# Transposes of W_down dealt out over the first two pairs of rows, with ScalarE's copies and two of GpSimd's steps at other places

## The reference

```
xn = layernorm(x)
s  = attention(xn, Wq, bq, Wk, bk, Wv, bv, gamma)
q4(t): per block of 16: scale = max|t| / 6; nearest of 0, .5, 1, 1.5, 2, 3, 4, 6 (with sign) * scale
h  = silu(q4(xn) @ q4(w_gate).T) * (q4(xn) @ q4(w_up).T)      # 704 wide
g  = silu(q4(h) @ q4(w_down).T)
out = x + s * g
```

## Time and profile before

| | before |
|---|---|
| median of 3 runs | 601.14 us (600.61 to 601.36) |
| the profiled execution | 601.82 us, of which its span is 599.7 us |
| TensorE (PE) busy | 549.6 us, 92% of the span |
| VectorE (DVE) busy | 557.2 us, 93% |
| ScalarE (ACT) busy | 416.1 us, 69% |
| GpSimd (POOL) busy | 258.9 us, 43% |

### The profile page before, as it was taken

How to read it: one execution, slowest core, us unless ns; L and a number is a source line. 1 busy time by engine, 2 the same in 40 slices (tenths; PEclk the granted TensorE clock), 3 DMA queues, 4 the chain that set the end, 5 groups by cost and what they waited for, 6 DMA issues and landing times. The chain is left out here.

```text
span 599.7 us, 15172 instructions
## 1 busy us (share of the span) xinstructions
PE 549.6 (92%) x4957; PEld 426.0 (71%) x4957; DVE 557.2 (93%) x1178; ACT 416.1 (69%) x901; POOL 258.9 (43%) x214
## 2 busy tenths in 40 slices
PE   0487799999999999999999989999999999999896
PEld 0355566777787777778787757778887777778775
DVE  7997999999999999999999997999999999977763
ACT  3978788878787776767776767777776776654421
POOL 6433333333443454335544344445644434423226
PEclk9999999999999999999999989999999999999999
DMA  8010000000011001111010111111011111122033
GB/s 249 18 37 19 19 20 19 19 19 19 19 37 37 19 2 55 55 54 54 31 48 33 54 57 55 55 54 29 28 55 54 54 37 37 36 100 96 0 124 142
DMA packets 17488, 29.14 MB, mean 49 GB/s; under 512 B 2688, under 2 KB 4864, under 8 KB 17408
## 3 DMA queue, kind: packets, MB, share of 16 engines
q1 hardware_dynamic: 17408, 28.13, 14.1%
HBM read 19.73 MB, written 8.39 MB: 47 GB/s over the span
## 5 line engine op out<-in xcount | busy, mean ns | idle before, releaser
L1414 PE MATMUL GU<-wgu,xqT 128*128 128x352 f16 x1536 | 252.6, 315 | 5.5 <-DVE h L941 2.1
L1414 PEld LDWEIGHTS GU<-wgu,xqT 128*128 128x128 f16 x1536 | 148.3, 99 | 79.7 <-issue 3.6
L545 POOL TENSOR_TENSOR ht<-h,hrr 128x1408 f32<-128x1408 f32 x32 | 82.9, 2591 | 82.8 <-DVE hrr L955 81.3
L629 ACT ACTIVATE sil<-GU,wkap 128x352 f32<-128x352 f32 x128 | 70.8, 554 | 59.8 <-PE GU L1414 58.9
L1424 PE MATMUL DS<-wdT,hqT 128*128 128x256 f16 x704 | 88.4, 275 | 1.9 <-ACT hqT L636 1.9
L941 DVE SCALAR_TENSOR_TENSOR h<-GU,wkap,sil 128x352 f32<-128x352 f32 x128 | 69.2, 540 | 13.6 <-ACT sil L629 9.7
L989 DVE TENSOR_TENSOR hq<-hg,hs 128x704 f16<-128x704 f16 x128 | 79.2, 659 | 1.0
L1424 PEld LDWEIGHTS DS<-wdT,hqT 128*128 128x128 f16 x704 | 67.2, 99 | 12.6 <-ACT hqT L636 2.3
L504 POOL TENSOR_TENSOR xnat<-xs,xnat 128x510 f16<-128x510 f32 (+1 forms) x32 | 37.0, 1159 | 89.9 <-DVE hq L989 81.6
L494 POOL TENSOR_TENSOR rs<-ve,half 128x2 f32<-128x2 f32 x32 | 23.1, 723 | 115.3 <-DVE ht L978 108.8
L665 ACT ACTIVATE gring<-DS,hun 128x256 f32<-128x256 f32 (+1 forms) x64 | 29.9, 467 | 44.9 <-issue 30.9
(11 more groups left out here) (166 smaller groups left out, 969.8 us busy)
## 6 DMA issues: line engine op xcount, KB each, us to landing
xin<-in_L_attn_x SPq DMA_DIRECT2D x34, 256.0 KB, 2.8
xe<-in_L_attn_x SPq DMA_DIRECT2D x25, 256.0 KB, 2.7
out<-o SPq DMA_DIRECT2D x25, 256.0 KB, 2.0
algebra<-in_L_ffn_w_down SPq DMA_DIRECT2D x1, 704.0 KB, 7.2
gring<-in_L_ffn_w_up SPq DMA_DIRECT2D x1, 640.0 KB, 5.8
xs<-in_L_attn_x SPq DMA_DIRECT2D x2, 256.0 KB, 3.9
xt<-in_L_attn_x SPq DMA_DIRECT2D x2, 256.0 KB, 4.5
out<-xin SPq DMA_DIRECT2D x2, 256.0 KB, 2.6
```

Source lines behind the costliest of these rows:

```text
L545: g.tensor_tensor(paired(ht[:, 0:2 * I]), paired(h[:, q]), spread(hrr[:, q], 4 * CB), ALU.mult).then_inc(S["ht_d"], 1)
L629: a.activation(sil[:, c], GU[:, c, 0, 0:CH], ACT.Silu, scale=wkap[:, 0:1]).then_inc(S["sil_d"], 1)
L1414: last = t.matmul(GU[:, c, m, 0:CH], xqT[:, k, j, 2 * a_ + kc], wgu[:, b_, kc, 2 * m + c], start=(z == 0 and kc == 0), stop=(z == 2 and kc ...
```

## The change

The transposes of W_down are dealt out over more places. Before, groups 0, 1, 2 stood in the first place of pair 0's second half, groups 3, 4 in the second place of that half, and group 5 in pair 1. Now groups 0, 1 stand in the first place, group 2 in the second, groups 3, 4 in the first half of pair 1, and group 5 in the second half of pair 1. A table DOWN_BANK names each group's bank of TR, and the waits follow from it. `rows_1` and `weights_v` go one pair later. ScalarE, in pair 1, copies groups 3 and 4 right behind the first silu, and `x_abs`, `h_high` and `h_abs` stand behind the second silu, ahead of `rows_out`. On GpSimd, `x_low` of pair 0 stands ahead of `x_rstd` and waits for the last copy of W_down's columns (`dupd`); `x_divide` of pair 0 waits for all four `h_mul` of the pair (`h_d` at 4). All the rest of the program is as it was, and the work is the same.

```diff
-        ASKS = {(-5, 0, 1): "rows_1", (-5, 1, 1): "weights_v", ...
+        ASKS = {(-4, 0, 1): "rows_1", (-4, 1, 1): "weights_v", ...
-        COPIES = {(-5, 1, 0): "rows_1", (-4, 0, 1): "weights_v", (2, 0, 1): "t1q", (3, 1, 0): "raw"}
+        COPIES = {(-4, 1, 0): "rows_1", (-3, 0, 1): "weights_v", (2, 0, 1): "t1q", (3, 1, 0): "raw"}
...
-        DOWN = {(0, 1, 0): (0, 1, 2), (0, 1, 1): (3, 4), (1, 0, 0): (5,)}
+        DOWN = {(0, 1, 0): (0, 1), (0, 1, 1): (2,), (1, 0, 0): (3, 4), (1, 1, 0): (5,)}
+        DOWN_BANK = (1, 0, 0, 1, 0, 1)
...  (GpSimd)
+                if isinstance(p, int) and p == 0:
+                    pool.wait_ge(S["dupd"], 4)
+                    x_low(p, k)
                 if on["xf"]:
...
-                    x_low(p, k)
+                        x_low(p, k)
                     if on["mb"]:
                         wait(pool, "hloq", 2 * p)
+                    else:
+                        pool.wait_ge(S["h_d"], 4)
                     x_divide(p, k)
...  (ScalarE)
+                if isinstance(p, int) and p == 1:
+                    down_out(p, 0, 0)
                 if on["xa"] and first:
                     x_norm(p, k)
                 attention(0, 0)
-                down_out(p, 0, 0)
+                second = isinstance(p, int) and p == 1
                 if on["h"]:
                     hidden_out(p, 0)
-                if on["xb"]:
+                if on["xb"] and not second:
                     x_abs(p, k)
                 if on["m"]:
                     silu(p, 0, 1)
+                if second:
+                    x_abs(p, k)
+                    h_high(p, k)
+                    h_abs(p)
...  (TensorE)
-                    pe.wait_ge(S["x_ev"], (2, 3, 3, 3, 4, 4)[i])
-                    if i >= 2:
-                        pe.wait_ge(S["w_ev"], GUR + i - 1)
+                    if i in (0, 1, 3):
+                        pe.wait_ge(S["x_ev"], (2, 3, 0, 4)[i])
+                    else:
+                        pe.wait_ge(S["w_ev"], GUR + (0, 0, 2, 0, 3, 4)[i])
...
-                if isinstance(p, int) and (p, j) in ((0, 1), (1, 0)):
-                    pe.wait_ge(S["w_ev"], GUR + (3 if p == 0 else 6))
+                if isinstance(p, int) and (p, j) in ((0, 1), (1, 0), (1, 1)):
+                    pe.wait_ge(S["w_ev"], GUR + {(0, 1): 1, (1, 0): 5, (1, 1): 6}[p, j])
```

More of the change, by code:

```diff
@@ L256, in spread_in_order @@
             return ap.rearrange("p (n e o) -> p n e o", o=1, e=2).broadcast_to([P, blks // 2, 2, BLK])
-        ASKS = {(-5, 0, 1): "rows_1", (-5, 1, 1): "weights_v", (-2, 1, 2): "gram0_0", (-1, 0, 1): "gram0_1", (-1, 1, 1): "gram0_2", (6, 1, 2): "gram0_0", (0, 0, 1): "gram0_3",
+        ASKS = {(-4, 0, 1): "rows_1", (-4, 1, 1): "weights_v", (-2, 1, 2): "gram0_0", (-1, 0, 1): "gram0_1", (-1, 1, 1): "gram0_2", (6, 1, 2): "gram0_0", (0, 0, 1): "gram0_3",
                 (0, 1, 2): "gram1_0", (1, 0, 0): "gram1_1", (1, 0, 2): "turn", (2, 0, 0): "t1q", (2, 0, 2): "t1k",
@@ L813, in down_out @@
                     a.copy(wdT[:, c0:c0 + nc_, n * P:(n + 1) * P],
-                           TR[:, (i + 1) % 2, 0:nc_ * P].rearrange("p (c m) -> p c m", m=P)).then_inc(S["w_ev"], 1)
+                           TR[:, DOWN_BANK[i], 0:nc_ * P].rearrange("p (c m) -> p c m", m=P)).then_inc(S["w_ev"], 1)
             def iteration(p, k, b=0, i=-1, tail=False):
@@ L846, in iteration @@
                     rows_out(p, k, 0, on["xn"], on["e"])
-                if on["mb"]:
+                if on["mb"] and not second:
                     h_high(p, k)
@@ L1340, in down_transposes @@
                     pe.wait_ge(S["dupd"], 4)
-                    pe.wait_ge(S["x_ev"], (2, 3, 3, 3, 4, 4)[i])
-                    if i >= 2:
-                        pe.wait_ge(S["w_ev"], GUR + i - 1)
+                    if i in (0, 1, 3):
+                        pe.wait_ge(S["x_ev"], (2, 3, 0, 4)[i])
+                    else:
+                        pe.wait_ge(S["w_ev"], GUR + (0, 0, 2, 0, 3, 4)[i])
                     for z in range(nc_):
-                        last = t.transpose(TR[:, (i + 1) % 2, z * P:(z + 1) * P], down_columns(n, c0 + z), id16[:, :])
+                        last = t.transpose(TR[:, DOWN_BANK[i], z * P:(z + 1) * P], down_columns(n, c0 + z), id16[:, :])
                     last.then_inc(S["w_tr"], 1)
```

## The result

The changed kernel took 596.42 us (median of 6 runs, 595.66 to 597.88) beside 600.50 for the kernel before (6 runs, 599.47 to 601.36): ratio 0.9931, 95% interval 0.9914 to 0.9948. That is 4.1 us faster, where 3.7 was forecast and 597.4 in absolute time. The profiled execution took 597.39 us, its span 595.3 (before: 601.82 and 599.7).

What follows compares the result with a forecast made beforehand. VectorE was taken to lead from L978 (rounding of h of pair 0) to the end; links ahead of it summed to L978 3.75 us earlier, so 601.14 - 3.7 = 597.4 us, range 596.4 to 599.2.

Steps and rivals of the forecast that it cites:

- the way to L978: Stretch ahead of VectorE's rounding of h of pair 0: L978 starts at 57.0 without a wait, 3.75 us earlier.
- level and range: Whole program: median before of 601.14 less 3.7 gives 597.4 us, range 596.4 to 599.2.
- The sum: Links up to L978 added up: 3.7 us faster, bounds 3.3 to 4.0; full gain (3.2 to 4.2) chance 0.62.
- VectorE leads behind L978: From L978 to the end the program follows VectorE like one rigid train, so L978's 3.75 us carry through.
- The fall of the clock in pair 1: After TensorE's 2.8 us wait for group 5's copy: costs 1.7, taken as covered; uncovered, about 599, chance 0.15.
- TensorE's hidden transposes: Pair 2: TensorE ready at 62.4 to 62.7, level with VectorE's 62.6, 0 to 0.1 us lost.
- the two later waits of 0.8: TensorE waits 0.8 us twice before 95 us, taken as cover for its lateness and the clock's fall.
- The ports: VectorE beside GpSimd: x_low delays L921 by 0.2; rival 1.0, gain 2.9, 598.2; ports or another link, chance 0.13.
- TensorE runs full from 95 on: Behind 95 us: given as the argument against phases shifting elsewhere and the gain coming to nothing (chance 0.06).
- the fall of the clock at the loop's turn: TensorE at the turn of the loop: 1.3 us on its row, may not recur, so the range reaches down to 596.4.

Runs made afterwards that it cites:

- the changed kernel with filler at the end: The changed kernel plus 22 and 8 unread matmuls on TensorE at its waits in the last batch: median 595.68 us, ratio to before 0.9926.
- first experiment: The kernel before with GpSimd's two edits alone (x_low behind dupd, x_divide of pair 0 behind the fourth h): ratio to before 0.9993.
- the last round: The changed kernel run again unaltered, beside the kernel before and both kernels with extra TensorE matmuls: median 597.57 us, ratio to before 0.9957.

## Why the prediction was right on the way to L978 and wrong in its level and range

**The way to L978 held link by link.** The changed trace is 0.47 early at the mark. With that added back, the measured starts stand beside the forecast so: `gate_up(0,1,1)` 45.06 (45.1), `gate_up(1,0,0)` 47.45 (47.4), silu 49.44 (49.4), second silu 53.36 (53.4), h 53.95 (54.0), L990 56.90 (57.0), without a wait. The sum was 3.75 and measured 3.89. Nearly all of the 0.14 is the piece from h to L978, taken as 3.04 and measured 2.95 (56.43 - 53.48), and rounding.

**VectorE leads behind L978.** Shown from both sides: 1.2 us more of VectorE came out at the end in full, 0.9 us more of TensorE, put where it had 1.21 to spare, not at all. But the train is rigid only from hq on. Between L978 and hq VectorE can still be held up by a silu: it waited 0.34 and 0.85 there in two variants, and hq came 0.5 and 0.6 later although L978 (L993 there) did not.

**The fall of the clock in pair 1 came and was covered,** as taken. TensorE's hidden transposes came at 63.38 + 0.47 = 63.85, 1.2 late against the 62.6, and of the two later waits of 0.8 one was left. The kernel without the fall was not faster. The cleanest pair is the changed kernel with GpSimd as before, where the clock stayed up behind this wait, and the changed kernel with filler at the end, where it fell behind the same wait:

```profile
59.72 0.38 PE L1400 MATMUL TR<-id,xq 128*128 128x128 f16 x4 [2.57 <-ACT wdT L814]
...
60.16 1.08 PE L1583 MATMUL G<-wqkv,ones 128*128 128x256 f32 x4
61.09 1.95 PE L1422 MATMUL GU<-wgu,xqT 128*128 128x352 f16 x12
```

```profile
58.76 0.38 PE L1405 MATMUL TR<-id,xq 128*128 128x128 f16 x4 [2.56 <-ACT wdT L819]
...
60.26 3.50 PE L1427 MATMUL GU<-wgu,xqT 128*128 128x352 f16 x12
```

From hq to the end these two took 532.6 and 532.4. At the turn of the loop it is alike: the two kernels with the copies behind h_abs waited 2.71 and 2.33 there, with a fall (the first product 2.67) and without one (1.96), and took 532.5 and 532.4 from hq to the end. The longest products there (3.25 and 3.51, in the traces of before and changed) may have cost a few tenths: from hq to mtop's product these two took 502.0, the others 501.5 to 501.9.

By the Trainium skill ("TensorE: Matmul & The Clock Gate", on HAM oscillation), idle gaps throttle TensorE again and the burst behind them starts cold. The changed kernel's trace agrees (2.02 against 1.08), the trace of the kernel with GpSimd as before (1.08 behind 2.57) does not.

**The ports.** L933 was held back 0.1, not 0.2. That GpSimd's edits carry 0.8 in the new order was right (0.88). In the old order they carry none (first experiment).

**What failed** is the last step, from the sum to the time: 601.14 - 3.7 = 597.4, with a range that ends at 596.4. It had no term for the clock at the end of the program, put at nothing with "TensorE runs full from 95 on", and for the low end I wrote that "the fall of the clock at the loop's turn (1.3 on its row) may not recur". That fall costs little or nothing. The one that matters is at the wait for mtop at the end of the last batch: 32.4 against 30.8 us, 1.55. TensorE does not run full there (it waits 1.45, 0.45 and, at 574.83 in before, 1.31). The profiled execution of before had the fall, and the three runs I was given (600.61 to 601.36) probably had it in whole or in part; the lower runs of the same kernel later lay at 599.3 to 600.3. I took 601.14 for the level of before, and it was the level of a mixture. Of the 0.98 us between 597.4 and 596.42, 0.64 is this level (600.50 with three more runs), 0.19 the sum (3.7 against 3.89), and the rest, 0.15, is left to how many runs of each kernel had the fall.

Set on the lower group, 599.8 - 3.9 = 595.9, a forecast with this in sight would have been two times, near 596 and near 597.5, and a range from 595.5. The trace had it on show: 0.50 of the clock at 569. That the medians came out 4.1 apart, near the 3.7, is in part luck, as they were 2.2 apart in the last round; the 3.89 of the traces and the 4.0 with filler are not.

That the three runs of before fell on one side or the other I can't show, since they have no traces. Why the clock falls behind the same wait in one execution and not in another stays open.

## What to carry to other kernels

Find the engine that is full without a wait and the first instruction from which it stays so; what lies ahead of that instruction could be summed here link by link to a tenth of a us, and what lies beside it is free until its cover is used up. Edits that did nothing in the old order (GpSimd's two, tried together) were worth 0.9 us in the new one, so an edit without effect is worth trying again once its neighbour has moved. If runs of one kernel scatter by more than a few tenths, cut the traces at common marks before you forecast a level: here one wait near the end made two kinds of runs, and 2.0 us of matmuls in idle time (1.39 and 0.61) brought them together.

## What the runs showed of the hardware

A gap of some 2 us on TensorE may or may not be followed by the lower clock: 2.08 at 63.23 was not (first product 1.95), and in the first experiment the same gap of 2.08 was:

```profile
62.77 3.49 PE L1419 MATMUL GU<-wgu,xqT 128*128 128x352 f16 x12 [2.08 <-DVE h L946]
```

At the end of the last batch it fell in four traces behind 1.45 and 0.45 us of waiting with two small float32 products between them, and in seven traces with the same waits it did not.

The hold-up between VectorE and GpSimd shows in both directions. L933 took 0.1 longer beside x_low, and GpSimd's step of two elements, which takes 0.70 elsewhere, took 1.14 when it started while L933 ran. In the kernel before it started 0.38 ahead of the same VectorE instruction (44.53 against 44.91) and took 0.70. The changed kernel:

```profile
43.53 1.16 POOL L505 TENSOR_TENSOR xnat<-xs,xnat 128x510 f16<-128x510 f32 x1 [1.80 <-DVE xnat L1223]
44.64 1.14 POOL L495 TENSOR_TENSOR rs<-ve,half 128x2 f32<-128x2 f32 x1
...
58.13 0.70 POOL L495 TENSOR_TENSOR rs<-ve,half 128x2 f32<-128x2 f32 x1 [4.83 <-DVE ht L990]
```

VectorE's reduction of h (1.62) was not longer with x_divide (48.08 to 49.14) beside it than without.
